# Three bias vectors of a cross-attention and FFN kernel: from matmul rows to additions on GpSimd, and the output weights staged elsewhere

## The reference

```python
x = x + L0_xattn(ctx, norm(x), mask)   # 4 heads: softmax(q k^T) v over 1024 latents + 77 context rows, @ Wo.T + bo (bo0)
x = x + L0_ffn(norm(x))                # two matmuls with gelu, low-rank terms, + b2 (b20)
x = x + L1_xattn(norm(x), ctx)         # 8 heads over the 77 context rows, @ Wo + bo (bo1)
x = x + L1_ffn(norm(x))                # 8 experts, each picks 257 tokens per batch row
```

## Time and profile before

| | us |
|---|---|
| median of 3 runs | 941.45 (941.11 to 944.87) |
| profiled execution, whole time | 941.11 |
| its span | 939.3 |
| PE / DVE / ACT / POOL busy | 797.3 / 545.7 / 400.4 / 336.3 |

### The profile page before, as it was taken

The page is one execution under the profiler, slowest core; times in us unless marked ns, Lnnn a source line. Parts: engine busy times, 40 slices in busy tenths (PEclk is TensorE's granted clock), DMA queues, the critical chain, the costliest instruction groups (busy, mean ns, idle before and its releaser), DMA issues.

```text
span 939.3 us, 12829 instructions
## 1 busy us (share of the span) xinstructions
PE 797.3 (85%) x4836; PEld 631.3 (67%) x4836; DVE 545.7 (58%) x1140; ACT 400.4 (43%) x721; POOL 336.3 (36%) x302
## 2 busy tenths in 40 slices
PE   2759988989999999988999887884159999899998
PEld 2536554655655555667789777883148988898897
DVE  5666686566576583355433487875835545564532
ACT  2324544454445334551431333323035654465563
POOL 5414101210220022153440042233245568566863
PEclk9859999999999999999999888996569999999999
DMA  6000000000000100100030201111211344144422
GB/s 167 1 0 1 1 1 1 1 1 1 1 1 0 46 3 0 45 1 3 1 86 1 90 1 46 46 46 51 96 45 26 118 139 132 25 132 136 138 27 24
DMA packets 21119, 39.44 MB, mean 42 GB/s; under 512 B 4491, under 2 KB 16641, under 8 KB 18753
## 3 DMA queue, kind: packets, MB, share of 16 engines
q1 hardware_dynamic: 14401, 30.18, 9.7%
q0 software_dynamic: 6656, 8.43, 5.0%
HBM read 30.06 MB, written 8.40 MB: 41 GB/s over the span
## 4 chain that ended last, share of the span: by engine, by line
PE 48%; DVE 22%; POOL 12%; issue 11%; ACT 5%; DMA 1%; SPq 0%; ACTq 0%; POOLq 0%; DVEq 0%
PE ps L439 14%; PE ps L578 9%; PE ps L678 5%; PE ps L1033 4%; DVE mx L1196 4%; POOL out_dram L2425 4%; POOL gt L2295 3%; PE ps L542 3%; PE ps L595 2%; PE ps L596 2%; POOL wh L2420 2%; DVE qkn L1155 2%; PE ps L519 2%; DVE oh L1652 1%; DVE rep L1584 1%
## 5 line engine op out<-in xcount | busy, mean ns | idle before, releaser
L578 PE MATMUL ps<-PT,VA 128*65 128x512 f32 (+1 forms) x288 | 147.7, 595 | 0.2 <-ACT PT L1820 0.2
L1033 PE MATMUL ps<-wh,he 128*128 128x256 f32 (+1 forms) x960 | 127.4, 289 | 0.0
L1033 PEld LDWEIGHTS ps<-wh,he 128*128 128x128 f32 (+1 forms) x960 | 111.8, 171 | 6.9
L1820 ACT ACTIVATE PT<-ps 128x512 f32<-128x512 f32 x128 | 76.0, 595 | 65.9 <-PE ps L596 65.4
L1196 DVE TENSOR_REDUCE mx<-ps 128x1 f32<-128x1104 f32 x64 | 83.5, 1305 | 34.4 <-PE ps L542 34.0
L439 PE MATMUL ps<-GT,wh 128*128 128x258 f32 x768 | 96.2, 286 | 2.6 <-ACT het L2094 1.5
L439 PEld LDWEIGHTS ps<-GT,wh 128*128 128x128 f32 x768 | 94.8, 193 | 3.7 <-ACT het L2094 1.9
L1686 DVE TENSOR_TENSOR he<-het,he 128x516 fp32r<-128x516 f32 x64 | 44.8, 700 | 59.6 <-ACT he L1712 52.4
L2146 POOL TENSOR_TENSOR rs<-rs,half 128x4 f32<-128x4 f32 (+2 forms) x19 | 17.7, 933 | 169.5 <-DVE rs L1069 158.0
L2425 POOL DMA_INDIRECT out_dram<-ye,idx x40 | 66.5, 1663 | 22.7 <-ACT ye L1712 15.7
L2155 POOL TENSOR_TENSOR ssq<-ssq,half 128x4 f32<-128x4 f32 x32 | 32.5, 1016 | 111.2 <-DVE ssq L1137 111.1
(11 more groups left out here) (259 smaller groups left out, 1560.2 us busy)
## 6 DMA issues: line engine op xcount, KB each, us to landing
wr<-in_w1e_dram SPq DMA_DIRECT2D x8, 1024.0 KB
wr<-in_w2e_dram SPq DMA_DIRECT2D x8, 1024.0 KB
x<-in_x_dram SPq DMA_DIRECT2D x4, 512.0 KB, 6.8
w<-in_w_dram SPq DMA_DIRECT2D x2, 1024.0 KB, 4.8
y_dram<-yr SPq DMA_DIRECT2D x3, 512.0 KB, 3.0
out_dram<-x SPq DMA_DIRECT2D x3, 512.0 KB, 4.3
b2e<-in_b2e_dram SPq DMA_DIRECT2D x8, 128.0 KB
gt<-y_dram,idx POOLq DMA_INDIRECT x40
```

The source lines that it names most:

```text
L578: pe.matmul(bank[6 + hf][0:65, :], VA[b][0:K, kt, h, :], PT[u % 4][0:K, :], start=kt == 0, stop=kt == 8).then_inc(p_pv, 1)
L1033: op = pe.matmul(bank[bk][0:M, 0:256], he[j][:, m, c0:c0 + M], w2h[i][:, 256 * m:256 * m + 256], start=n == 0, stop=n == 23)
L1820: a.activation(PT[u % 4][0:K, :], bank[4 + u % 2][0:K, :], ACT.Exp, bias=0.0 if K == 128 else mcol[:, b:b + 1]).then_inc(a_exp, 1)
```

## The change

One tile `rows` [128, 3, 256] holds all three vectors on all 128 partitions. POOL adds `bo0` (`add_row(0, g)`) to each group behind its first norm, `b20` as before (`add_row(1, g)`), and `bo1` (`add_row(2, g)`) behind the norm of L1 attention. `row1`, `row2`, `one` and the matmuls with `one` go. `wo_in` moves out of `OT`'s place into a part of `qkn`, and its split moves ahead of the projections on ACT and on POOL.

```diff
+        rows = R0("rows", [128, 3, D])
-        wo_in = Arena(ot_at)("wo_in", [65, H0, 258])[:, :, :]
+        wo_in = qkf[0:65, 1536:1536 + 1032].rearrange("p (k n) -> p k n", k=H0)
 # tensor_program, values_out
-                        pe.wait_ge(d_rows, 32)
-                        pe.wait_ge(g_one, 2)
...
-                                op = pe.matmul(bank[m][:, 0:256], one[:, :], row1[:, :], start=False, stop=True)
 # vector_program: proj (P == 0), wo_tile, ffn2, product
-                            v.wait_ge(a_whi, 2)
-                            v.wait_ge(g_wlo, 2)
+                            v.wait_ge(a_whi, 3)
+                            v.wait_ge(g_wlo, 3)
...
+                if hi % 4 == 0 and qt == 0:
+                    v.wait_ge(g_row, 2 * b + 2)
...
-                        v.wait_ge(g_row, g + 1)
+                        v.wait_ge(g_row, 4 + g + 1)
...
-                    v.wait_ge(a_z, n // 4 + 1)
+                    v.wait_ge(g_row, 8 + n // 4 + 1)
 # scalar_program
-                    elif hf == 0:
-                        a.wait_ge(g_wlo, 3)
...
             copy(wv[0], wv_in).then_inc(a_whi, 1)
             for _ in range(5):
                 next(first)
+            a.wait_ge(g_wo, 1)
+            a.wait_ge(d_w, 144)
+            copy(wo[0], wo_in).then_inc(a_whi, 1)
...
-            a.wait_ge(g_wo, 1)
-            a.wait_ge(d_w, 160)
-            copy(wo[0], wo_in).then_inc(a_whi, 1)
 # gpsimd_program
-            def add_row(g):
+            def add_row(i, g):
                 g_.tensor_tensor(x[:, 4 * g:4 * g + 4, :], x[:, 4 * g:4 * g + 4, :],
-                                 row2[:, :].unsqueeze(1).to_broadcast([128, 4, D]), ALU.add).then_inc(g_row, 1)
+                                 rows[:, i:i + 1, :].to_broadcast([128, 4, D]), ALU.add).then_inc(g_row, 1)
...
             def norm_n(g):
                 yield from idle(2)
                 factors(("n", g), 4 * g, 4)
                 yield
+                yield
+                g_.wait_ge(a_z, g + 1)
+                add_row(2, g)
+                yield
...
-            g_.memset(one[:, SC:128], 0.0).then_inc(g_one, 1)
-            g_.wait_ge(g_one, 1)
-            g_.memset(one[:, 0:SC], 1.0).then_inc(g_one, 1)
-            g_.wait_ge(g_one, 2)
...
-            step(g_.memset(wo_in[64:65, 1:H0, 0:256], 0.0))
+            step(g_.memset(wo_in[64:65, :, :], 0.0))
             settle()
             g_.memset(wo_in[64:65, :, 256:257], 1.0).then_inc(g_wo, 1)
             g_.wait_ge(g_wo, 1)
+            g_.wait_ge(a_whi, 3)
+            g_.tensor_tensor(wo[1], wo_in, f(wo[0]), ALU.subtract).then_inc(g_wlo, 1)
             root_q(0, 0)
...
             scale_qk(0, 1)
-
-            g_.wait_ge(a_whi, 3)
-            g_.tensor_tensor(wo[1], wo_in, f(wo[0]), ALU.subtract).then_inc(g_wlo, 1)
+            g_.wait_ge(d_rows, 48)
+            g_.wait_ge(v_z, 2)
+            add_row(0, 0)
+            add_row(0, 1)
+
             proj(1)
             for g in (2, 3):
                 factors(("ln", g), 4 * g, 4)
+                g_.wait_ge(v_z, g + 1)
+                add_row(0, g)
 # sync_program
-            sp.dma_start(wo_in[64:65, 0, 0:256], A["bo0"].partition_broadcast(1)).then_inc(d_w, 16)
-            sp.dma_start(row2[:, :], A["b20"].partition_broadcast(128)).then_inc(d_rows, 16)
-            sp.dma_start(row1[:, :], A["bo1"].partition_broadcast(1)).then_inc(d_rows, 16)
+            for i, n in enumerate(("bo0", "b20", "bo1")):
+                sp.dma_start(rows[:, i, :], A[n].partition_broadcast(128)).then_inc(d_rows, 16)
```

More of the change, by code:

```diff
@@ L113, in build @@
         rs = R0("rs", [128, NT])
-        row2 = R0("row2", [128, D])
-        row1 = R0("row1", [1, D])
-        one = R0("one", [1, 128])
+        rows = R0("rows", [128, 3, D])
         yb = [R0(f"yb{i}", [128, 4, D]) for i in range(2)]
@@ L157, in build @@
         PT = [RA(f"PT{i}", [128, 512]) for i in range(4)]
-        ot_at = RA.at
         OT = [RA(f"OT{j}", [65, S], F32R) for j in range(2)]
-        wo_in = Arena(ot_at)("wo_in", [65, H0, 258])[:, :, :]
         rec = RA("rec", [128, 8])
@@ L290, in build @@
         g_init = sem("g_init")
-        g_one = sem("g_one")
         g_st = sem("g_st")
@@ L468, in ctx @@
                 if b == 0:
-                    pe.wait_ge(d_w, 160)
+                    pe.wait_ge(d_w, 144)
                 pe.matmul(bank[m][0:SC, :], ctxT[:, 0, 0:SC], wc[:, 0, :], start=True, stop=False)
@@ L746, in values_out @@
                                                VD[:, 616 * q + 128 * c:616 * q + 128 * c + M], wo1[:, q, :],
-                                               start=q == qs[0], stop=q == qs[-1] and c > 0)
-                            if c == 0:
-                                op = pe.matmul(bank[m][:, 0:256], one[:, :], row1[:, :], start=False, stop=True)
+                                               start=q == qs[0], stop=q == qs[-1])
                         op.then_inc(p_vw, 1)
@@ L1499, in vector_program @@
                 next(first)
-            v.wait_ge(d_w, 160)
+            v.wait_ge(d_w, 144)
             v.scalar_tensor_tensor(gg[:, 2:3], gg[:, 0:1], DH ** -0.5, gg[:, 1:2], ALU.mult, ALU.mult)
@@ L2161, in scale_qk @@
                     if P == 0:
-                        g_.wait_ge(a_whi, 2)
-                        g_.wait_ge(g_wlo, 2)
+                        g_.wait_ge(a_whi, 3)
+                        g_.wait_ge(g_wlo, 3)
                     else:
@@ L2188, in lnf @@
                 g_.wait_ge(v_z, 4 + g + 1)
-                add_row(g)
+                add_row(1, g)
             def w1_lora(b):
@@ L2346, in gpsimd_program @@
             proj(3)
-            g_.wait_ge(d_rows, 32)
             lnf(0)
```

## The result

The changed kernel took 951.57 us (median; 949.5 to 953.76 in four timed runs), the kernel before 941.28 (940.39 to 944.87). The ratio is 1.0102, 95% interval [1.0061, 1.0143]: slower by 5.7 to 13.5 us. A repetition in twelve runs (first experiment) gave 1.009 [1.0052, 1.0128]. Forecast were 950.4 and slower.

What follows compares the result with a forecast made beforehand. The chain of waits at each addition's place, not POOL's 36% average load, was taken to bound it. Terms 0.4 + 4.8 + 1.6 - 1.1 + 1.8 + 1.8 = +9.3 on 941.11 gave 950.4 us; 8-in-10 range 945 to 955.

Steps and rivals of the forecast that it cites:

- (a): Start-up: `wo` split ahead of the projections delays DVE's second cast, +0.4 us; removing it later gains nothing.
- (b): Behind `scale_qk(0, 1)`: two back-to-back POOL additions hold DVE's waiting operations until both end, +4.8 us.
- (c): Beside `ln(1)`: additions for groups 2 and 3 delay two DVE casts on the chain, +1.6 us.
- (d): L1 attention: removing the bias matmuls, two per batch row, shortens the chain, -1.1 us.
- (e): L1 attention: `add_row(2, 2)` delays `normed(3)`, and PE's transposes of tile 3 wait for it, +1.8 us.
- (f): Routing: `add_row(2, 3)` ahead of POOL's inverse root starts that root late, +1.8 us.
- a lower clock as well: Rival, 954 us: PE's new idle stretches lower its clock, 1.0 us each, up to four; chance 0.14.
- By the pair at 749.71 DVE gets neither in before the end: At about 50 us: POOL keeps its turn through both additions, so lines 1189 and 1155 wait, +4.8 us.
- hand-over at each end: Rival, 948.0 us: the waiting engine gets in whenever the other finishes, so the first two additions cost 2.4; chance 0.13.
- the cheaper alternative: Routing: the row behind the inverse root (line 1445) may lose its hold, so the late start costs only 0.8 us.
- PE's transposes of tile 3 [...] wait for it: L1 attention: transposes, at 559.53 before, wait until 561.35 for `normed(3)`, held behind `add_row(2, 2)`, +1.8 us.
- next late is `nmr`: L1 attention: behind the second removed matmul pair, `nmr` is next late by 0.5 us, as POOL's inverse root ends at 527.17.

Runs made afterwards that it cites:

- experiment 1: The changed kernel again, same text, twelve runs: median 955.56 us, ratio 1.009 to the kernel before.
- 5: The kernel before with only the `wo` split moved early, ahead of the projections: 941.09 us, ratio 0.9994.
- 2: The changed kernel with its first two additions waiting until DVE's product (line 1145) is done: 948.17 us, ratio 1.0059 to the kernel before.
- experiment 3: The changed kernel with its first two additions cut into eight of 128x256 at the same place: 946.38 us, ratio 1.0037 to the kernel before.
- 9: The changed kernel with only `add_row(0, 2)` and `add_row(0, 3)` moved later, away from DVE's casts: 947.29 us, ratio 1.0024 to the kernel before.
- 6: The kernel before without the four bias matmuls, `bo1` left out altogether: 941.59 us, ratio 1.0012.
- 7: The changed kernel with only the last two additions, `add_row(2, 2)` and `add_row(2, 3)`, moved later: 946.9 us, ratio 1.0055 to the kernel before.
- experiment 4: The changed kernel with six additions, the four of `bo0` and the last two of `bo1`, moved later: 940.17 us, ratio 0.9974 to the kernel before.
- 8: The kernel before with `bo1` alone on POOL, its last two additions moved later: 942.35 us, ratio 0.9994.
- 10: The kernel before with `bo1` alone on POOL, at the places where the change puts it: 945.32 us, ratio 1.0.

## Why the prediction came out right, step by step

The time was right, 951.57 against 950.4, but that was luck in part: the steps of the order were put 3.5 us too high, and the clock, which the sum leaves out, made up for it. The steps of the order, as the traces have them, against the forecast:

| step | forecast | measured | from |
|---|---|---|---|
| (a) `wo` split early | +0.4 | +0.3 | the casts; 5 |
| (b) `add_row` (0,0), (0,1) | +4.8 | +2.0 | line 1145; 2, 3 |
| (c) (0,2), (0,3) | +1.6 | +1.5 | casts; 9 |
| (d) bias matmuls gone | -1.1 | -1.4 | 6 |
| (e) (2,2) | +1.8 | +1.6 at full clock, +0.5 beside a low one | 1, 2; 7 |
| (f) (2,3) | +1.8 | +1.8, and 0.3 to 0.9 behind it | line 1434; 7 |
| sum | +9.3 | +5.8, +4.7 with (e) at 0.5 | |

The sum of 5.8 agrees with the 5.6 us that experiment 1 shows between the kernels at equal clock (good to about 1, so it agrees with 4.7 as well). What filled the gap up to its 11.1 us goes with the clock, another 5.5 us on average. That was the rival "a lower clock as well", which was priced at 4 us on top of a sum that was itself too large.

**(b) is the term that was mis-sized.** It failed at the words "By the pair at 749.71 DVE gets neither in before the end". DVE got both in: the short one at the end of `scale_qk`, the long one at the end of the first addition. That is the rival "hand-over at each end", a little cheaper than it said (2.0, not 2.4). Line 1179 delayed no addition: the first began at 49.47, 0.15 before that row's end, and took 2.34. And DVE's product, which was waiting, needed only 1.09 behind it instead of its usual 1.24. The Trainium skill ("SBUF — State Buffer", section "SBUF: two separate sides") says that the port pair is an exclusive lock, held for the whole instruction, and that a DVE operation with two SBUF inputs contends for it. By that rule the trace agrees: 3.27 us on DVE are 2.18 of waiting and 1.09 of work, and POOL's second addition waits in its turn. Who is next the page doesn't say; here it was the one that waited.

At 749.71 it was POOL that went on, and that was no accident: DVE's line 1652, 1.2 us by itself, takes 3.75 to 3.78 in six of its sixteen places in the trace of before, each time beside such a pair of POOL, and the same line does so six times in the changed kernel. The pair of the earlier trace rows, each operation by itself:

```profile
749.71 1.86 POOL L2420 TENSOR_TENSOR wh<-wr,wh 128x512 fp32r<-128x512 f32 x1
...
750.99 1.81 POOL L2420 TENSOR_TENSOR wh<-wr,wh 128x512 fp32r<-128x512 f32 x1
```

POOL's second operation starts here 0.58 us ahead of the end of the first (751.57), while the second addition at 51.77 starts only 0.04 ahead of it, and the second small piece of experiment 3 as well (0.03). Other differences: the pair stands behind an indirect DMA issued by POOL, and DVE's operation is in bf16, while around 50 us all are float32 operations of 128x1024. Which of these decides wasn't tried and stays open. So the prediction read its row rightly; what failed was to carry it over to another pair.

**(c), (f)**: right in place and size, each because a row of before showed what stood beside the addition. For (f) the state of the rows was kept (line 1437 still 1.17), not the cheaper alternative.

**(e)**: the order was counted right, `normed(3)` came 5.89 us later than before, of which this execution was 2.25 late already at 554 (DVE's line 1397), so 3.64 by the step; 3.87 were forecast. "PE's transposes of tile 3 [...] wait for it" holds where the clock is full: PE waits 1.53 and 1.51 us in experiments 1 and 2, and DVE loses 1.6. In the first trace PE was late at 563.2 by its own low clock in that stretch and waited 0.22 us. Two delays side by side count once: there the step adds 0.5 to the 1.1 to 1.2 that 4, 6, 7 and 8 lose at the low clock without it. The prediction's sum had no term for that.

**(d)**: 1.36 instead of 1.1, as each pair of matmuls was worth 0.8 and not 0.62. The answer "next late is `nmr`" was right (it now waits for POOL). In the traces of 4, 6 and 8 most of it is lost again at tile 3, where their clock was 0.72 to 0.75 and that of before 1.00.

**The clock.** Forecast as four stretches of 1 us behind PE's new idle time. One of these is shown: behind `(2,3)`. Where that addition is early, DVE loses 0.8 to 0.9 us there in four traces (first, 3, 9, 10) and 0.3 in two (1, 2); where it isn't, 0.1 or less (4 to 8). The largest, 437 to 455, is not of that kind: kernels 5 and 10 have it with hardly anything of the change ahead of it, and experiment 4, with all twelve additions, doesn't have it in its trace. Whether the change makes low stretches likelier stays open. For it: experiment 1 has the lowest mean clock of all (0.920, before 0.929), and two of its twelve runs reach 0.930. Against: experiments 3 and 9 keep most of the change and have 0.930.

## What to carry to other kernels

Bound an addition to a lightly used engine by its place, not by its share: twelve additions cost nothing once six of them had been moved by one wait or a few steps, and 5.6 us in the places next to them. When DVE and POOL want the same thing, one instruction of the other is the likelier price than its whole queue, but not a sure one: around 50 us it was one, beside the pairs like that at 749.71 it was both. Work out both prices and look at the row. Where the POOL instruction can't be moved, cutting it in pieces shortened DVE's hold from 2.03 to 0.41 us. Where runs of one kernel differ by 14 us with the granted clock, compare times at equal clock, and only with runs of the other kernel made beside them, before reading a difference of a few us into an edit: at equal clock one kernel still differed by 3.1 us between sets. And read a step in more than one trace: `(2,2)` showed 0.5 us in two of them and 1.6 in two others.

## What the hardware showed that was not expected

- POOL's back-to-back additions of float32 don't keep DVE out: DVE's held product ran between them (3.27 us with pieces of 2.34, 1.65 with pieces of about 0.7), and POOL's next piece waited about 0.9 to 1.0 us for it. Its pairs in the experts' loop do keep DVE out (3.75 to 3.78 us instead of 1.2, six times).
- A matmul pair whose row shows 0.62 us moved the reader behind it by 0.8 when it was taken out. Why it is more than the row wasn't looked into.
- One kernel, one chip: 946.3 to 960.7 us, with mean clock 0.933 and 0.907 in the same twelve runs. In the L0 FFN a stretch of 18 us at 0.62 (0.92 in before) put DVE 4.3 us back.
